# A factorization machine on one core: entries dealt to partitions in runs of 16 or 8 in place of 4, and the last tile of x in four pieces

## What is computed

```python
B, VOCAB, F = (512, 6250, 64)        # x: int32 zeros and ones, V: fp32, bias: fp32
xv = xf @ V
sum_sq = jnp.sum(xv * xv, axis=-1)
sq_sum = xf @ jnp.sum(V * V, axis=-1)
second_order = 0.5 * (sum_sq - sq_sum)
linear = g_bias + xf @ bias
return linear + second_order[:, None]
```

## Time and profile before

| | |
|---|---|
| Time, median of three runs | 48.98 us (48.85 to 49.02) |
| The profiled execution's own time | 49.03 us |
| Its span, first to last instruction | 47.2 us |
| DVE busy | 30.5 us (65% of the span) |
| PE busy | 22.0 us (46%) |
| POOL busy | 20.5 us (43%) |
| ACT busy | 13.7 us (29%) |
| DMA, bytes as written | 4.87 MB |

### The profile page before, as it was taken

One profiled execution on the slowest core, in us unless ns is written; L12 is line 12 of the kernel. 1 busy time (PEld: TensorE's weight loads), 2 busy tenths in 40 slices (PEclk: granted clock), 3 DMA queues, 4 the chain that ended last, 5 costly groups with the idle time before them and its releaser, 6 DMA issues.

```text
span 47.2 us, 634 instructions
## 1 busy us (share of the span) xinstructions
PE 22.0 (46%) x210; PEld 20.1 (43%) x210; DVE 30.5 (65%) x74; ACT 13.7 (29%) x30; POOL 20.5 (43%) x34
## 2 busy tenths in 40 slices
PE   0000000000000000045999995999999999997200
PEld 0000000000000000045989893998999899985100
DVE  2000000000999469997999899999999999998600
ACT  0000009100899469954996300020002000000000
POOL 1999800000199009999599999990000000000000
PEclk9999999999999999999999999999999999999998
DMA  0399999999999999999999999999999970000000
GB/s 0 102 152 100 109 140 152 164 189 158 175 174 172 181 170 178 146 142 108 105 106 106 106 106 106 101 104 103 116 96 101 94 55 3 0 0 0 0 2 0
DMA packets 5583, 4.87 MB, mean 103 GB/s; under 512 B 1434, under 2 KB 5581, under 8 KB 5581
## 3 DMA queue, kind: packets, MB, share of 16 engines
q0 software_dynamic: 3456, 3.21, 73.4%
q1 hardware_dynamic: 1155, 0.82, 6.7%
q10 hardware_dynamic: 970, 0.81, 5.3%
HBM read 14.48 MB, written 0.00 MB: 307 GB/s over the span
## 4 chain that ended last, share of the span: by engine, by line
DVE 42%; DMA 34%; ACTq 10%; issue 4%; PE 2%; ACT 1%
DMA v_in<-in_L_rec_V_dram 34%; DVE x_all L330 13%; DVE seen L344 13%; ACTq L150 5%; DVE v_rest L295 3%; ACTq L237 3%; DVE xv L354 3%; DVE w_sum L301 2%; DVE xv_sq L359 2%; DVE odd_turned L335 2%; PE xv_ps L466 2%; ACTq L233 2%; DVE seen L406 1%; ACTq L234 1%; DVE seen L350 1%
## 5 line engine op out<-in xcount | busy, mean ns | idle before, releaser
L466 PE MATMUL xv_ps<-wall,x_all 128*128 128x195 bf16 x192 | 19.9, 266 | 1.8 <-DVE x_all L330 1.8
L466 PEld LDWEIGHTS xv_ps<-wall,x_all 128*128 128x128 fp8e4 x192 | 18.0, 105 | 2.7 <-DVE x_all L330 1.1
L160 POOL DMA_DIRECT2D x_all<-in_r_x_dram x24 | 13.0, 551 | 0.8 <-POOLq L498 0.8
L216 POOL TENSOR_TENSOR wall<-v_rest 128x512 bf16<-128x512 f32 (+1 forms) x6 | 7.4, 1247 | 10.2 <-DVE v_rest L295 10.2
L450 PE MATMUL g_ps<-g_in,ones 1*128 1x1 f32 x2 | 0.6, 342 | 20.2 <-DMA g_in<-in_L_rec_g_bias_dram 20.2
L450 PEld LDWEIGHTS g_ps<-g_in,ones 1*128 1x128 f32 x2 | 0.5, 305 | 20.2 <-issue 20.2
L330 DVE STREAM_TRANSPOSE x_all<-x_all 128x512 uint32<-128x512 uint32 (+1 forms) x13 | 8.5, 652 | 0.0
L364 DVE MEMSET v_in<- 22x64 f32 x1 | 0.1, 112 | 10.6 <-DMA v_in<-in_L_rec_V_dram 10.6
L344 DVE TENSOR_TENSOR seen<-seen,x_all 128x512 uint32<-128x512 uint32 (+1 forms) x10 | 6.3, 628 | 0.0
L251 ACT ACTIVATE v_sq<-v_in 128x512 f32<-128x512 f32 (+1 forms) x6 | 3.8, 636 | 5.3 <-DVE v_in L364 3.5
L295 DVE TENSOR_TENSOR v_rest<-v_in 128x512 f32<-128x512 f32 (+1 forms) x6 | 4.3, 750 | 1.4 <-DMA v_in<-in_L_rec_V_dram 1.3
(11 more groups left out here) (27 smaller groups left out, 9.5 us busy)
## 6 DMA issues: line engine op xcount, KB each, us to landing
x_all<-in_r_x_dram POOLq DMA_DIRECT2D x12, 196.0 KB, 9.7
v_in<-in_L_rec_V_dram ACTq DMA_DIRECT2D x6, 128.0 KB, 13.3
v_in<-in_L_rec_V_dram SPq DMA_DIRECT2D x6, 128.0 KB, 11.3
x_all<-in_r_x_dram POOLq DMA_DIRECT2D x4, 100.0 KB, 7.4
x_all<-in_r_x_dram POOLq DMA_DIRECT2D x4, 64.0 KB, 8.5
x_all<-in_r_x_dram POOLq DMA_DIRECT2D x4, 32.0 KB, 8.1
bias_in<-in_L_rec_bias_dram ACTq DMA_DIRECT2D x3, 6.5 KB
v_in<-in_L_rec_V_dram SPq DMA_DIRECT2D x1, 24.0 KB
```

What stands on the lines that cost most here:

```text
L160: queue.dma_start(x_words[S * i:S * i + S, t, :, lo // QUAD:hi // QUAD].bitcast(fp8), rows[:, :, START[i] + lo:START[i] + hi]).then_inc(x_ ...
L216: nc.gpsimd.tensor_tensor(placed(n, 2), v_part(v_rest, n), upper(v_rest, n), ALU.subtract).then_inc(low_placed, 1)
L466: last = nc.tensor.matmul(xv_ps[t][:, :, :], rows[:, q, :], wall[:, 1 + QUAD * d + q, :, 0:E], start=(d + q == 0), stop=(d == ND - 1 and q ...
```

## The change

Load 0 and load 1 of V (quads 0 to 3, 4 to 7) are dealt in runs of 16 entries: a block of 4 quads is 512 entries, 16 in a row to each partition. Load 2 (quads 8 to 11) is dealt in runs of 8 over 2 quads. A partition's part of a V transfer is then one run of 4 KB, or two of 2 KB. The bias is dealt in the same way straight to its place `bias_in[P, NC]`, in runs of 64 B or 32 B, by `load_bias`: four transfers for quads 0 to 7 and four for quads 8 to 11, besides four of 128 B for the odd rows. VectorE's wait is for all 12. The second bias transpose goes. The words of x are transposed with a stride, as a run of 4 words (or 2) now belongs to one partition; a turn can't cross a block, so each tile has turns of 4, 4, 2 and 2 quads in place of 4, 4 and 4, and tile 3 has pieces of 4, 4, 2 and 2 quads. The order on VectorE has one more turn and one more check in tile 0.

```diff
-    PIECES = [(t, 0, ND) for t in range(T - 1)] + [(T - 1, 0, 6), (T - 1, 6, 10), (T - 1, 10, ND)]
-    TURNS = [(k, t, d, min(d + 4, d1)) for k, (t, d0, d1) in enumerate(PIECES) for d in range(d0, d1, 4)]
+    PIECES = [(t, 0, ND) for t in range(T - 1)] + [(T - 1, 0, 4), (T - 1, 4, 8), (T - 1, 8, 10), (T - 1, 10, ND)]
+    PARTS_D = [(0, 4), (4, 8), (8, 10), (10, 12)]
+    TURNS = [(k, t, a, b) for k, (t, d0, d1) in enumerate(PIECES) for a, b in PARTS_D if d0 <= a and b <= d1]
     V_LOADS = [(0, 4), (4, 8), (8, 12)]
+    V_PART = [4, 4, 2]
+    BIAS_LOADS = [(0, 8, 4), (8, 12, 2)]
...
     def load_v(queue, n, quarters):
         d0, d1 = V_LOADS[n]
+        sizes = dict(c=S, j=QUAD * V_PART[n])
         for i in quarters:
             queue.dma_start(
-                v_in[S * i:S * i + S, 1 + QUAD * d0:1 + QUAD * d1, :].rearrange("c (d q) f -> c d (q f)", q=QUAD),
-                V[START[i] + S + d0 * W:START[i] + S + d1 * W, :].rearrange("(d c q) f -> c d (q f)", c=S, q=QUAD)
+                v_in[S * i:S * i + S, 1 + QUAD * d0:1 + QUAD * d1, :].rearrange("c (s j) f -> c s (j f)", j=sizes["j"]),
+                V[START[i] + S + d0 * W:START[i] + S + d1 * W, :].rearrange("(s c j) f -> c s (j f)", **sizes)
             ).then_inc(v_landed[n], 16)
+
+    def load_bias(queue, n):
+        d0, d1, size = BIAS_LOADS[n]
+        for i in range(NQ):
+            queue.dma_start(
+                bias_in[S * i:S * i + S, 1 + QUAD * d0:1 + QUAD * d1].rearrange("c (s j) -> c s j", j=QUAD * size),
+                bias[START[i] + S + d0 * W:START[i] + S + d1 * W, :].rearrange("(s c j) o -> c s (j o)", c=S, j=QUAD * size)
+            ).then_inc(bias_landed, 16)
...
     load_v(act, 0, (2, 3))
     act.wait_ge(bias_cleared, 1)
-    act.dma_start(bias_in[0:1, W - S:W], bias[0:S, :].rearrange("l o -> o l")).then_inc(bias_landed, 16)
-    act.dma_start(bias_in[1:1 + ND, :], bias[S:Q, :].rearrange("(d l) o -> d (l o)", l=W)
-                  ).then_inc(bias_landed, 16)
-    for i in range(1, NQ):
-        act.dma_start(bias_in[S * i:S * i + 1 + ND, :],
-                      bias[START[i] + S - W:START[i] + Q, :].rearrange("(d l) o -> d (l o)", l=W)
+    for i in range(NQ):
+        act.dma_start(bias_rows[S * i:S * i + 1, :], bias[START[i]:START[i] + S, :].rearrange("l o -> o l")
                       ).then_inc(bias_landed, 16)
+    load_bias(act, 0)
     load_v(act, 1, (2, 3))
     load_v(act, 2, (2, 3))
+    load_bias(act, 1)
     act.dma_start(g_in[:, :], g_bias.rearrange("(a b) -> a b", b=1)).then_inc(g_landed, 16)
...
     nc.vector.transpose(x_turned[:, t, d0:d1, :].rearrange("p d (g r) -> p d g r", r=S),
-                        turn_words(u).rearrange("p g (d c) -> p d g c", c=S)).then_inc(x_turned_ready, 1)
+                        turn_words(u).rearrange("p g (c d) -> p d g c", c=S)).then_inc(x_turned_ready, 1)
...
-    dve.wait_ge(bias_landed, 16 * (NQ + 1))
+    dve.wait_ge(bias_landed, 16 * NQ * (1 + len(BIAS_LOADS)))
...
-    nc.vector.transpose(bias_turned[:, :, :], bias_in[:, :].rearrange("p (c q) -> p q c", q=QUAD)
-                        ).then_inc(bias_turned_ready, 1)
...
     keep_rest(4)
     keep_rest(5)
     turn(1)
+    turn(2)
     sum_squares(4)
     sum_squares(5)
     weigh(2)
     turn_odd(0)
-    turn(2)
+    turn(3)
     check(1)
     check(2)
+    check(3)
```

More of the change, by code:

```diff
@@ L77, in factorization_machine @@
         wall = sb("wall", [P, NC, PARTS, STRIDE], bf16)
-        bias_in = sb("bias_in", [P, W], fp32)
-        bias_turned = sb("bias_turned", [P, QUAD, S], fp32)
+        bias_in = sb("bias_in", [P, NC], fp32)
+        bias_rows = sb("bias_rows", [P, S], fp32)
         bias_odd = sb("bias_odd", [P, S], fp32)
@@ L163, in gen_steps @@
         def gen_steps(loop, step):
[L164 to L167, removed]
+            n = 0
+            for a, b, size in BIAS_LOADS:
+                with loop(0, (b - a) // size) as s:
+                    for d in range(size):
+                        for q in range(QUAD):
+                            k = d * QUAD + q
+                            part = x_in[:, :, bass.ds(s * (size * W) + (S + a * W), size * W)]
+                            step(s * (QUAD * size) + (n + k), part.rearrange("p g (c j) -> p j g c", c=S)[:, k],
+                                 s * (QUAD * size) + (n + k + 1))
+                n += QUAD * (b - a)
             step(NC - 1, x_in[:, :, 0:S], 0)
@@ L287, in _ @@
         def _(dve):
-            nc.vector.memset(bias_in[:, :], 0.0).then_inc(bias_cleared, 1)
+            nc.vector.memset(bias_rows[:, :], 0.0).then_inc(bias_cleared, 1)
             nc.vector.memset(ones[:, :], 1.0).then_inc(consts_set, 1)
@@ L308, in weigh @@
                 if n == 0:
-                    dve.wait_ge(bias_turned_ready, 2)
+                    dve.wait_ge(bias_turned_ready, 1)
                     nc.vector.scalar_tensor_tensor(w_all[:, 0:1], w_sum[:, 0:1], -0.5, bias_odd[:, 0:1],
                                                    ALU.mult, ALU.add).then_inc(w_ready, 1)
-                nc.vector.scalar_tensor_tensor(w_all[:, quads].rearrange("p (d q) -> p d q", q=QUAD),
-                                               w_sum[:, quads].rearrange("p (d q) -> p d q", q=QUAD), -0.5,
-                                               bias_turned[:, :, 1 + d0:1 + d1].rearrange("p q d -> p d q"),
+                nc.vector.scalar_tensor_tensor(w_all[:, quads], w_sum[:, quads], -0.5, bias_in[:, quads],
                                                ALU.mult, ALU.add).then_inc(w_ready, 1)
@@ L366, in _ @@
             keep_rest(1)
-            dve.wait_ge(bias_landed, 16 * (NQ + 1))
-            nc.vector.memset(bias_in[last_quarter:last_quarter + 1, W - S:W - S + OVER], 0.0
-                             ).then_inc(overlap_cleared, 1)
+            dve.wait_ge(bias_landed, 16 * NQ * (1 + len(BIAS_LOADS)))
+            nc.vector.memset(bias_rows[last_quarter:last_quarter + 1, 0:OVER], 0.0).then_inc(overlap_cleared, 1)
             dve.wait_ge(overlap_cleared, 2)
-            nc.vector.transpose(bias_odd[:, :], bias_in[:, W - S:W]).then_inc(bias_turned_ready, 1)
-            nc.vector.transpose(bias_turned[:, :, :], bias_in[:, :].rearrange("p (c q) -> p q c", q=QUAD)
-                                ).then_inc(bias_turned_ready, 1)
+            nc.vector.transpose(bias_odd[:, :], bias_rows[:, :]).then_inc(bias_turned_ready, 1)
             sum_squares(0)
@@ L455, in _ @@
                     pe.wait_ge(low_placed, d1 // 2)
-                    pe.wait_ge(w_placed, PARTS * (d1 // 4))
+                    pe.wait_ge(w_placed, PARTS * -(-d1 // 4))
                 if d1 == ND:
```

## The result

The changed kernel takes 64.22 us (median of 4 runs, 63.88 to 64.31) against 49.0 us (48.85 to 49.21): a ratio of 1.306, interval 1.296 to 1.316. Its profiled execution took 63.88 us, with a span of 62.1 us against 47.2. The direction was forecast, the size was not: 57.7 us was said, with a range of 54 to 60.

The account below looks back on a forecast made before the run. VectorE's own list was taken to bound the kernel from 13.38 us. Bias landing 23.2 + list 30.1 = 53.3, + 2.64 = 55.9 span, + 1.83 outside, less 0.05: 57.7 us, 18% slower; range 54.0 to 60.0.

Parts of the forecast that it names:

- The bias gate: VectorE waits at L367 for the whole bias ahead of load 0's sums; landing 21.4 to 24.1 us, 23.2 taken.
- The count of turns: DMA queues alternate one packet each; ACT's queue needs 64 turns on the slowest engine, or 58 if odd rows spread.
- the rival with 0.09: Runs of one transfer share a DMA turn: about 38 turns, bias at about 18 us, time 52.6 us; chance 0.09.
- the rival "faster": Bias is no gate, landing at 13 us: 47.5 us, chance 0.05; break-even if it lands by 14.5 us.
- V, ScalarE and x: V load 0 lands at 8 to 9 us, ACT's first square starts at 11.2, x is in time by 4 us.
- GpSimd's side of the supply: GpSimd issues x tile 2 at about 27.6 us, not 19.12; tile 3's 16 transfers are issued by 42.1.
- VectorE's list: VectorE's work from L368 to its end: 31.2 - 1.3 - 0.3 + 0.5 = 30.1 us, ending at 53.3.
- the stride term: Extra cost of VectorE's strided turns: 0 to 0.5 ns an element, 0 to 3.1 us over 6144 elements.
- I take 0: Choice of no cost for the strided turns, as L372's single duration was not trusted.
- The upper bound of 3.1 us: Most the strided turns could cost: 0.5 ns an element on the 6144 elements of all turns.
- the rival's 0.14: Chance of the slower case: strided turns cost 0.5 ns an element, up to 3.1 us more, 60.8 us.
- 2.64 (from VectorE's end to the span's end): Tail after VectorE's last instruction, 47.23 - 44.59 in the kernel before, added to 53.3 for a 55.9 us span.

Follow-up runs that it names:

- the kernel with runs of 8: Kernel before with all entries dealt in runs of 8 (V in 2 KB), bias rows of 1 KB, general path 2 steps long: 47.72 us, ratio 0.968.

## Why the prediction was wrong, step by step

**The bias gate: right.** The count of turns gave 21.4 to 24.1 us with 23.2 as likeliest, and VectorE was released at 23.23; moved in front of V it gave 18 to 19.5, and 18.22 was measured. That it fits to the tenth is luck: the same count was 0.9 us off for the kernel before, and no row shows whether the slowest engine had 64 turns or 58. The doubt whether short runs of a transfer share a turn is settled by the 68 to 68 packets: they do not, and the rival with 0.09 falls. So does the rival "faster": nothing came near a landing by 14.5 us. Rows 7, which the forecast held against shared turns, had not settled it even for V: x and V both had 9 packets for each engine and transfer, so turns of a whole transfer's share would have given equal counts too. The bias has 5 against the 9 of x.

**V, ScalarE and x: right.** V load 0 landed at 8.86 ("8 to 9"), the first square started at 11.01 (11.2). The second is luck: ACT had 7 transfers more to issue ahead of its table load (12 for 5), not 6, and rows 6 give 0.53 us for each (11 from 0.74 to 6.62), not 0.45; the load came 2.6 us later (9.61 for 6.98), near the 2.7 of the forecast. GpSimd's side of the supply, on its timeline:

```profile
27.54 2.18 POOL L173 DMA_DIRECT2D x_all<-in_r_x_dram  x4
...
33.78 8.65 POOL L173 DMA_DIRECT2D x_all<-in_r_x_dram  x16
```

27.54 against 27.6, and the last issue ends at 42.4 against 42.1. The DMA engines stood idle between, as the stretches show (DMA share and GB/s last), and VectorE never waited for x:

```profile
23.00:28.00 5.00, 0.50 (x2) 0.41 (x2) 4.60 (x13) 2.90 (x7) 1.83 (x2) 1.00 0.00 0
```

**VectorE's list: the stride term was mis-sized.** The step that failed is "I take 0". The list was put at 30.1 us and measured 33.1. The only row with a stride, the bias transpose of rows 3, gave 0.5 ns an element and was set aside because other durations near it were disturbed. It was the right row: 0.8 ns was measured for the turns at a stride of four words. The bias transpose of the kernel with runs of 8 says the same, 597 ns for 256 elements at a stride of eight words, where 256 without a stride take 438. The upper bound of 3.1 us was right in size by two errors that cancel, all 6144 elements at 0.5 ns where it is 4096 at 0.8 ns and 2048 at nothing. The likeliest value should have been the row's and not the lower end, and the rival's 0.14 should have been the forecast.

**The end: a term that was not in the sum.** "2.64 (from VectorE's end to the span's end)" was carried over as a constant. The diff itself multiplies `gen_steps` by five on three engines, and I left it out since it is never executed. It cost 3.2 us, the wait of TensorE's branch for its instructions. With both terms as measured the sum is 57.8 + 3.0 + 3.2 = 64.0 for the profiled execution, which took 63.88. The range failed for the same reason: the stride's price went into its upper end by half, and the path not at all.

## What to carry to other kernels

When queues share DMA engines with a long stream, price a transfer by its turns, data packets and closing packets, and place its wait where its data is used: here 25 KB of bias in runs of 32 and 64 B held up 33 us of work by 10 us, and splitting the wait gave back 9 us. A layout that makes transfers longer has to be paid where it is read; check how many bytes lie between two elements that an engine takes one after the other. And read the diff for code that is never run: a branch over it can have to wait for instructions.

## What was not expected of the hardware

- VectorE's transpose of 512 words takes 0.69 us at strides of 4 and 8 bytes, and 1.06 to 1.11 us at every stride tried from 16 to 48 bytes.
- TensorE's taken branch costs 0.37 us over 5 or 13 steps of code, 4.5 to 4.8 us over 25, and ends 1.3 us after a transfer of instructions has landed. The other engines' branches over their share of the same steps stayed short (45 to 72 ns in the changed kernel).
- One packet a turn holds down to 32 B, which was forecast, but from no row with runs this short: in the same microsecond, 68 packets of x's queue, all but one of which read 6272 B, and 68 of the bias queue.
